# Making the low parts of two weights in four GpSimd operations each instead of one, in a transformer layer in split float32

## What is computed

```python
x = x + layernorm(attn(layernorm(x)))   # 16 heads of 32, causal, biases on q, k, v and out
x = x + layernorm(ffn(layernorm(x)))    # silu(h @ gate.T) * (h @ up.T), then down; inner size 2048

# attn, for its input h
q, k, v = h @ q_w.T + q_b, h @ k_w.T + k_b, h @ v_w.T + v_b      # each weight 512 x 512
p = softmax(where(causal, q k.T / sqrt(32), -inf))
attn = (p v) @ o_w.T + o_b
```

## Time and profile before

| | us |
|---|---|
| median of 3 runs | 1028.7 |
| lowest and highest | 1028.31 and 1029.04 |
| profiled execution, own time | 1027.8 |
| its span in the trace | 1026.0 |

### The profile page before, as it was taken

How to read it: one execution, slowest core, us unless ns; L and a number is a source line. 1 busy time by engine, 2 the same in 40 slices (tenths; PEclk the granted TensorE clock), 3 DMA queues, 4 the chain that set the end, 5 groups by cost and what they waited for, 6 DMA issues and landing times.

```text
span 1026.0 us, 15720 instructions
## 1 busy us (share of the span) xinstructions
PE 980.4 (96%) x5669; PEld 754.7 (74%) x5669; DVE 720.4 (70%) x1418; ACT 410.4 (40%) x717; POOL 691.2 (67%) x498
## 2 busy tenths in 40 slices
PE   5998999999999999998898999999999999999997
PEld 4766676766776776755576888888888888888886
DVE  6676777887597777875778577776665877777722
ACT  4215455555215555554335233332543433333232
POOL 4204888799535999999266976653688768776273
PEclk8999999999999999999899999999999999999999
DMA  6232333323421333231132222111432322211043
GB/s 224 78 88 58 96 83 89 87 76 78 134 82 35 93 88 89 73 95 42 62 112 96 93 76 77 62 62 44 161 113 93 112 77 74 98 62 62 20 154 134
DMA packets 49182, 90.70 MB, mean 88 GB/s; under 512 B 10448, under 2 KB 10960, under 8 KB 48848
## 3 DMA queue, kind: packets, MB, share of 16 engines
q1 hardware_dynamic: 48560, 89.43, 28.7%
q10 hardware_dynamic: 544, 0.26, 0.1%
HBM read 55.84 MB, written 8.39 MB: 63 GB/s over the span
## 4 chain that ended last, share of the span: by engine, by line
PE 75%; DVE 11%; POOL 7%; ACT 2%; issue 2%; DMA 2%; SPq 1%; POOLq 0%; ACTq 0%; DVEq 0%
PE ps L1649 19%; PE ps L1651 18%; PE ps L1650 18%; PE ps L1744 6%; PE ps L1715 5%; PE ps L1778 5%; POOL p_sum L747 3%; PE ps L1792 1%; DVE p_sum L1268 1%; DVE xt_lo L1282 1%; DMA x_in<-x 1%; POOL p_sum L743 1%; POOL p_sum L740 1%; DVE stats L1444 1%; PE ps L1752 1%
## 5 line engine op out<-in xcount | busy, mean ns | idle before, releaser
L1305 DVE CUSTOM_DVE_ANT_0 ps<-ps,mask_q 128x384 f32<-128x384 f32 (+7 forms) x256 | 189.9, 780 | 67.9 <-PE ps L1715 65.0
L1744 PE MATMUL ps<-q_stack,k_stack 98*128 98x512 f32 (+3 forms) x384 | 117.0, 382 | 9.4 <-ACT p_own L982 3.3
L1715 PE MATMUL ps<-k_stack,q_stack 96*128 96x512 f32 (+3 forms) x384 | 108.9, 364 | 1.6 <-DVE m_full L1305 0.9
L769 POOL TENSOR_TENSOR dn_lo<-dn_raw,dn_hi 128x512 fp32r<-128x512 f32 x48 | 65.7, 1370 | 47.2 <-ACT dn_hi L1074 47.2
L1744 PEld LDWEIGHTS ps<-q_stack,k_stack 98*128 98x128 f32 x384 | 62.7, 192 | 33.7 <-ACT p_own L982 8.3
L1715 PEld LDWEIGHTS ps<-k_stack,q_stack 96*128 96x128 f32 x384 | 66.6, 192 | 27.1 <-DVE m_full L1305 11.4
L814 POOL TENSOR_TENSOR gu_lo<-s_raw,gu_hi 128x1024 fp32r<-128x1024 f32 x27 | 64.8, 2402 | 23.2 <-ACT gu_hi L1145 23.2
L982 ACT ACTIVATE p_own<-ps 128x512 f32<-128x512 f32 x112 | 61.0, 598 | 42.8 <-PE ps L1744 23.7
L982 ACT ACTIVATE x_in<-ps 128x512 f32<-128x512 f32 x112 | 60.9, 598 | 36.5 <-PE ps L1744 20.4
L1168 ACT ACTIVATE silu<-ps 128x512 f32<-128x512 f32 x27 | 16.2, 599 | 141.5 <-DVE ps L1540 141.5
L810 POOL TENSOR_TENSOR a_lo<-gu_raw,a_hi 128x512 fp32r<-128x512 f32 x27 | 35.8, 1327 | 51.8 <-ACT a_hi L1138 51.7
(11 more groups left out here) (224 smaller groups left out, 2827.8 us busy)
## 6 DMA issues: line engine op xcount, KB each, us to landing
gu_raw<-gu_w SPq DMA_DIRECT2D x37, 512.0 KB, 3.6
dn_raw<-dn_w SPq DMA_DIRECT2D x48, 256.0 KB, 2.6
x_in<-x SPq DMA_DIRECT2D x32, 256.0 KB, 4.4
q_stack<-st_hi SPq DMA_DIRECT2D x128, 64.0 KB, 2.0
k_stack<-st_hi SPq DMA_DIRECT2D x128, 64.0 KB, 2.0
qk_raw<-qk_w SPq DMA_DIRECT2D x16, 256.0 KB, 3.0
q_stack<-st_lo SPq DMA_DIRECT2D x64, 64.0 KB, 2.0
k_stack<-st_lo SPq DMA_DIRECT2D x64, 64.0 KB, 2.0
```

The source lines that it names most:

```text
L769: nc.gpsimd.tensor_tensor(dn_lo[:, s], dn_raw[:, s], dn_hi[:, s].bitcast(F32), ALU.subtract).then_inc(dn_split, 1)
L1305: nc.vector.tensor_tensor_reduce(out=scores, in0=scores, in1=mask_q[:, SEQ - (t + 1) * P:], scale=1.0, scalar=MASKED, op0=ALU.add, op1=ALU ...
L1715: last = nc.tensor.matmul(bank[:, 0:width], q_stack[0:QK_ROWS, s, h, t * P:(t + 1) * P], k_stack[0:QK_ROWS, s, h, half * CH:half * CH + wi ...
L1744: last = nc.tensor.matmul(bank[:, at_col:at_col + n * P], k_stack[0:ROWS, s, h, kt * P:(kt + 1) * P], q_stack[0:ROWS, s, h, t * P:(t + n) ...
```

## The change

POOL makes each of the two low parts in four operations of 128x512, one per block, in place of one of 128x2048. Each of the four counts `vo_split` up by one, so the waits for 1 and 2 become waits for `KT` (4) and `2 * KT` (8).

```diff
@@ POOL
             for n, (hi, lo) in enumerate(((vw_hi, vw_lo), (ow_hi, ow_lo))):
                 pool.wait_ge(vo_hi_done, n + 1)
-                nc.gpsimd.tensor_tensor(lo[:, :, :], vo_raw[:, n], hi[:, :, :].bitcast(F32), ALU.subtract).then_inc(vo_split, 1)
+                for k in range(KT):
+                    nc.gpsimd.tensor_tensor(lo[:, k, :], vo_raw[:, n, k, :], hi[:, k, :].bitcast(F32), ALU.subtract).then_inc(vo_split, 1)
@@ SP
-            sp.wait_ge(vo_split, 1)
+            sp.wait_ge(vo_split, KT)
...
-            sp.wait_ge(vo_split, 2)
+            sp.wait_ge(vo_split, 2 * KT)
@@ PE
-                        pe.wait_ge(vo_split, 1)
+                        pe.wait_ge(vo_split, KT)
...
-            pe.wait_ge(vo_split, 2)
+            pe.wait_ge(vo_split, 2 * KT)
```

## The result

| | before | changed |
|---|---|---|
| median us (20 runs each) | 1027.78 | 1026.20 |
| lowest and highest | 1026.64 and 1029.77 | 1024.93 and 1028.57 |
| profiled execution, own time | 1027.8 | 1025.3 |
| its span | 1026.0 | 1023.5 |

The ratio is 0.9985, with a 95% interval of 0.9979 to 0.9992. The change makes the kernel 1.6 us faster, clear of the noise, but still inside the 0.2% that the prediction called "no change". 3.1 us were forecast. The time forecast, 1025.6, is 0.6 us off.

A forecast was written before the change was run, and what follows sets the result against it. PE, busy 980.4 of 1026.0 us, was taken as the bound, so only its waits could change: 1.5 us (data path) plus 1.6 us (clock) off 1028.7 gave 1025.6 us, range 1023.8 to 1027.6.

The forecast's parts named there:

- The reading of the stalls: DVE's normalising operations for tiles 4 and 8 (2.73, 2.31 us) stand still until POOL's long operation ends, plus 0.29 us.
- Does DVE get in between two pieces?: At POOL's seams DVE waits only for the running piece; tile 4 ends at 18.91, tile 5 at 21.56 us.
- Rival 2: Slower: DVE waits for all four queued POOL pieces; 1029.7 us, or 1031.3 with another low clock stretch; chance 0.07.
- V0: PE's matmuls after tile 5's transposes start 1.46 us earlier, but half clock leaves 0.73 us; X7 starts at 30.3.
- The term of 1.5 us for the data path: With DVE's second stall gone, P(0,0) on PE starts at 32.3 instead of 33.81 us, the 0.73 us included.
- rival 3: More gain: the clock may not fall near 21.0, V0 runs at full clock; 1.4 us more, 1024.2 us; chance 0.17.
- The clock behind it: PE's pause before P(0,0) shrinks from 2.17 to about 1.4 us, so P(0,0) runs at full clock: 1.63 us.
- Rival 1: The clock falls anyway on P(0,0) or P(0,1), so only 1.5 us are won: 1027.2 us; chance 0.22.
- I take no fall: Before P(0,0), a 1.4 us pause is nearer 0.97 (no fall) than 2.17 (fall); bounds 0 and 1.63 us.
- Against the median: The profiled execution lay 0.9 us under the median of the runs shown, so 3.1 us came off 1028.7.
- The covers: Later ends of POOL's low parts and of load_qk(1) (22.7 us) stay hidden; failing, up to 0.6 us comes back.
- It all moves along: Everything after P(0,0), from SP's copies and tile 13's load to the end, comes earlier by the full 3.1 us.

The follow-up runs named there:

- e3: Changed kernel with only the value weight's low part in four POOL operations, the output weight's in one: 1026.84 us, ratio 0.9987 to the kernel before.
- e4: Changed kernel with only the output weight's low part in four POOL operations, the value weight's in one: 1027.28 us, ratio 0.9993 to the kernel before.
- e6: The changed kernel profiled once more without any edit: one execution, 1025.12 us.
- e5: The kernel before profiled once more without any edit: one execution, 1026.63 us.
- e9: Changed kernel with two POOL operations of 128x1024 per weight in place of four: 1026.19 us, ratio 0.9986 to the kernel before.
- e10: Changed kernel with eight POOL operations of 128x256 per weight in place of four: 1025.59 us, ratio 0.9972 to the kernel before.
- e8: Changed kernel with PE's start pauses filled by idle matmuls, plus 14 before tile 13, where PE has no pause: 1026.45 us, ratio 0.9982 to the kernel before.
- e11: Changed kernel with 10 to 14 idle matmuls in PE's start pauses, none before tiles 6, 7, 13: 1024.32 us, ratio 0.9959 to the kernel before.
- e12: As e11, with ten more idle matmuls before the first scores of units 0 and 8: 1023.41 us, ratio 0.9955 to the kernel before.

## Why the prediction was right, and where it was off

- **The reading of the stalls: right.** e3 and e4 show that each long DVE operation goes with its own weight's POOL operation.
- **"Does DVE get in between two pieces?": right.** Tile 4 is done at 19.15 (18.91 forecast), tile 5 at 21.77 (21.56). The start of this execution runs 0.2 us later already (16.29 for 16.10). Rival 2 (slower) is out: with two, four and eight pieces, no wait of DVE was longer than one piece and 0.29 us. For tile 8 the wait depends on where in a piece DVE arrives (0.55 us in one execution, 1.57 in e6), which the bound of one piece covered.
- **"V0": right in kind.** The low clock did eat part of the early start. It lasted until 25.3 instead of 24.3, so X7 started at 30.77, not 30.3, and P(0,0) at 32.79, not 32.3. The term of 1.5 us for the data path was thus 1.0 us in this pair of profiles (33.81 to 32.79) and 1.3 in e5 against e6 (34.10 to 32.80). The other side of the coin, rival 3 (V0 at full clock), showed in e9 and e10 with tile 12's transposes at 48.7 and 48.9, but its 1.4 us went again at 85 and 317 us.
- **"The clock behind it": the step that was mis-sized.** I took the fall on P(0,0) for a fixed cost of before, 1.63 us, since the one trace had it. In that pair of profiles the term came in full: P(0,0) took 2.87 us in place of 4.47. But in e5 the same kernel before ran P(0,0) in 2.88 us and took 1026.63 us in all; there the term is nothing. Rival 1 and the sentences around it allowed for falls that differ between executions, but gave them a price only in the changed kernel, not in the one before.
- **What the term is worth in the median: an estimate only.** Ten of the 20 times of before lie from 1026.6 to 1027.5, the other ten from 1028.1 to 1029.8, none between. If these were executions without and with the fall, a removed fall would be worth about half of 1.63 in the median: 1.5 + 0.8 = 2.3 us. 1.6 us were measured, so even this leaves 0.7 us open. Nor are the groups that clean: of the 66 further times of before taken beside the experiments (one more, of 2434.49 us, is left out), nine lie between 1027.5 and 1028.1. The ten of the 66 with a mean granted clock of 0.991 took 1026.5 to 1027.1 us and the eleven with 0.981 or less 1028.5 to 1031.4; the 45 between took 1026.5 to 1029.7. And the changed kernel's own times reach from 1024.9 to 1028.6, while its two profiled executions took 1025.3 and 1025.1. No profile shows what its slower executions do.
- **"I take no fall": right, by luck in part.** The argument was that a pause of 1.4 us is nearer to 0.97 (no fall) than to 2.17 (fall). But the same trace held a third low stretch in the start, which the earlier trace rows does not show, and the pauses ahead of it were no longer than that: 1.43 us ahead of 11.67 and 1.26 us ahead of 14.02.

```profile
14.02 1.04 PE L1670 MATMUL ps<-ident,p_sum 128*128 128x128 f32 x4 [1.26 <-DVE p_sum L1268]
```

```profile
14.20:17.50 3.30, 2.85 (x14) 2.05 (x14) 2.90 (x7) 2.94 (x4) 1.40 (x1) 0.50 0.53 150
```

  In e3, on the other hand, no fall came on P(0,0) after 2.06 us. The length of the one pause ahead of it does not tell whether the clock falls.
- **"Against the median": off by 0.9 us.** The three runs shown (median 1028.7) all lay in the upper half of the 20; over 20 runs before is at 1027.78. That is why the forecast time is nearer than the forecast gain.
- **The covers held.** SP issued `load_qk(1)` at 22.94 (22.7 forecast), and ACT waited 1.74 us for its data, but ACT's next `xt_hi` copy, at 27.77, waited 1.20 us for PE anyway.
- **"It all moves along": right at the end of P(0,0)** (2.62 us by then, 2.47 us at the end of the span), in the pair of profiles compared. In e8 and e9 the lead of the start did not last, as told above.

## What to carry to other kernels

When a DVE operation that works on SBUF alone takes several times its usual time and ends 0.3 us after a long GpSimd operation, cut the GpSimd operation: here 1.05 us more on POOL (5.20 + 5.20 against 4.58 + 4.77) took 3.3 us off three DVE operations (0.72 + 0.99 + 0.55 against 2.73 + 0.55 + 2.31), and 2.3 us in e6. Before an effect of the clock is entered as a term, profile two or three executions of the same kernel: a fall that only some of them show is worth only its share of the executions. Follow a lead to the end of the span, too: in e8 and e9 a lead won in the first 50 us was partly lost at 85 and 317 us. And put idle matmuls only where PE has a pause.

## What the runs showed of the hardware

- DVE's operation got its turn at the next seam between queued GpSimd operations for pieces of 128x256, 128x512 and 128x1024 alike (the longest waits made it 1.00, 1.57 and 1.11 us long), and the POOL operation behind the seam lost about 0.2 us (1.46 in place of 1.27 to 1.28). This bears out the Trainium skill ("SBUF — State Buffer", the section on the two sides) with the lock ending at each instruction.
- Not every DVE operation is held up. In the kernel before, the moments, which also read and write SBUF only, took their usual 0.68 us in the middle of `vw_lo` (16.10 to 20.68), just ahead of the operation that took 2.73:

```profile
17.26 0.68 DVE L1264 BATCH_NORM_STATS2 stats<-x_in 128x6 f32<-128x512 f32 x1
```

- A seam itself is cheap: 0.62 us for three more operations (5.20 against 4.58), 1.39 us for seven more (5.97), DVE's turns included.
- In the start of the kernel before, the low clock stretches began near 14.1, 21.0 and 34.7 us in one execution and near 19.6 in another, which took 1.2 us less. This agrees with what the Trainium skill ("TensorE: Matmul & The Clock Gate", Part 1) says of a free-running monitor. In the changed kernel two executions had them at the same places. The mean granted clock alone does not give the time: before took 1027.8 us at 0.986 and 1026.63 at 0.988, the changed kernel 1025.32 at 0.988 and 1025.12 at 0.986.
- Four idle matmuls where PE has no pause cost 0.44 us of PE's path (from one start to the next, 30.33 to 30.77 in the changed kernel). With 10 to 14 of them in PE's pauses the clock was at 1.00 from 8.5 to 50 us in e11's profile, and up to 49 us in e12's. That the filling is the cause was not shown: in e9, without it, the clock was at 1.00 from 8.5 to 80 us too.
